# Keeping the row of "same source" flags in bf16 instead of f32: row in memory, preparation tile and scan operand

## The reference, cut to what matters

```
x = ln(x + H W0 + b0)            H = [x, A x, A A x, A A A x]      A z = segment_sum(w * z[dst], src)
x = ln(x + mlp([x, sum, max, mean of the edges' attributes by dst, u]))
x = ln(x + attention over the edges by dst + skip)
x = ln(x + (x + 3 A x) / 4)
```

## The kernel before, in words

| stage | about (us) | what runs in it |
|---|---|---|
| preparation | 0 to 400 | sorting, flags, index tables |
| node rows alone | 400 to 880 | first 48 node groups |
| A | 880 to 1780 | 100 node groups, and the first product (gathers from `in_x_rows`) for 100 edge groups |
| B | 1780 to 2540 | the last 52 node groups, and the second product (gathers from `Z1E`) for 100 edge groups, two for each node group |
| C | 2540 to 3740 | rows of sources: third product (gathers from `Z2E`), layers 1 and 2, attribute scans |
| D | 3740 to 4850 | rows of destinations |
| attention | 4850 to 6050 | third layer |
| last | 6050 to 7560 | fourth layer: gathers, product, scatters |

## Time and profile before

### The profile page before, as it was taken

One profiled execution on the slowest core, in us unless ns is written; L12 is line 12 of the kernel. 1 busy time (PEld: TensorE's weight loads), 2 busy tenths in 40 slices (PEclk: granted clock), 3 DMA queues, 4 the chain that ended last, 5 costly groups with the idle time before them and its releaser, 6 DMA issues.

```text
span 7577.1 us, 104573 instructions
## 1 busy us (share of the span) xinstructions
PE 4996.8 (66%) x26540; PEld 3423.6 (45%) x26540; DVE 4566.0 (60%) x8424; ACT 2745.5 (36%) x5600; POOL 4815.5 (64%) x4823
## 2 busy tenths in 40 slices
PE   0088799997777799999888988777777611111111
PEld 0055566665555677777644444444444311010100
DVE  8855577776666688888533333588888732222222
ACT  0044455554444344444322222377777500000000
POOL 0054566644656576666477777577777677777777
PEclk9999999999999899999899999888888755555555
DMA  0022466666999798888655555433333322222221
GB/s 15 13 82 84 116 196 195 196 197 170 217 224 219 209 257 252 252 250 251 173 155 148 150 154 155 118 108 107 109 109 107 85 65 66 65 66 65 66 65 57
DMA packets 871313, 1058.31 MB, mean 140 GB/s; under 512 B 144418, under 2 KB 505776, under 8 KB 871078
## 3 DMA queue, kind: packets, MB, share of 16 engines
q1 hardware_dynamic: 717578, 805.42, 34.4%
q0 software_dynamic: 153600, 251.49, 16.2%
HBM read 613.72 MB, written 454.66 MB: 141 GB/s over the span
## 4 chain that ended last, share of the span: by engine, by line
DVE 26%; PE 24%; issue 16%; POOL 16%; ACT 7%; DMA 6%; DVEq 5%; SPq 1%; ACTq 0%; POOLq 0%
PE bank L942 10%; POOL gat L645 7%; PE bank L844 5%; POOL xT L645 5%; DVE x L1661 4%; POOL out_rows L658 4%; PE bank L928 3%; DVE ln3vr L1649 2%; DVE t L1722 2%; ACT mbuf L1085 2%; PE bank L931 2%; DMA Z2E<-zE 2%; DMA gat<-X,d_x 2%; PE bank L930 2%; DVEq L1838 2%
## 5 line engine op out<-in xcount | busy, mean ns | idle before, releaser
L844 PE MATMUL bank<-ident,gat 128*128 128x128 f32 x2400 | 452.4, 319 | 1476.1 <-DVE zT L1690 1370.3
L1085 ACT ACTIVATE mbuf<-t 128x512 f32<-128x512 f32 x500 | 315.7, 631 | 2094.3 <-DVE t L1902 1351.9
L844 PEld LDWEIGHTS bank<-ident,gat 128*128 128x128 f32 x2400 | 311.8, 165 | 1633.2 <-issue 1285.3
L942 PE MATMUL bank<-W2s,hT 128*128 128x128 f32 x6400 | 875.7, 293 | 0.0
L1671 DVE TENSOR_TENSOR gat<-gat,pays 128x512 f32<-128x512 f32 x400 | 273.0, 682 | 993.4 <-DMA gat<-X,pays 955.2
L942 PEld LDWEIGHTS bank<-W2s,hT 128*128 128x128 f32 x6400 | 796.6, 203 | 94.5 <-issue 94.5
L928 PE MATMUL bank<-x1T,W1x 128*128 128x512 f32 x1600 | 803.5, 615 | 25.1 <-ACT x1T L1077 16.2
L671 POOL DMA_INDIRECT pays<-PAY,s_q x400 | 379.4, 948 | 626.2 <-DMA PAY<-payl 338.0
L844 PE MATMUL bank<-ident,x 128*128 128x128 f32 x3200 | 512.0, 284 | 236.1 <-DVE x L1661 231.3
L645 POOL DMA_INDIRECT gat<-in_x_rows,pays x400 | 395.0, 987 | 369.7 <-PE bank L844 264.9
L1141 ACT ACTIVATE hT<-bank,b1u 128x512 f32<-128x512 f32 x800 | 506.6, 687 | 256.8 <-PE bank L931 251.8
(11 more groups left out here) (342 smaller groups left out, 11849.2 us busy)
## 6 DMA issues: line engine op xcount, KB each, us to landing
X<-x SPq DMA_DIRECT2D x700, 256.0 KB, 3.9
fB<-row_s_same SPq DMA_DIRECT2D x400, 256.0 KB, 5.3
xT<-in_x_fm SPq DMA_DIRECT2D x200, 256.0 KB
out_rows<-x SPq DMA_DIRECT2D x200, 256.0 KB
ffB<-rows_last_notlast SPq DMA_DIRECT2D x100, 512.0 KB
Z1T<-zT SPq DMA_DIRECT2D x100, 256.0 KB, 2.1
Z1E<-zE SPq DMA_DIRECT2D x100, 256.0 KB
Z2T<-zT SPq DMA_DIRECT2D x100, 256.0 KB, 10.0
```

Source lines behind the costliest of these rows:

```text
L844: mm = pe.transpose(dst[:, t, :], tiles[t], ident[:, :])
L942: mm = pe.matmul(bMLP[:, t, :], hT[h][s][:, t * P:(t + 1) * P], W2s[:, h, :], start=False, stop=h == HC - 1, skip_group_check=True)
L1085: act.activation(sq[k % 3][s % 2], [bT1, t2[s], bSK, t2[s]][k][:, :, :], ACT.Square).then_inc(S(f"squared{k}", s), 1)
```

## The change

The flag row is kept in bf16, two bytes instead of four. 0 and 1 are exact in bf16. Four places change: the row in HBM, the preparation tile `ssame` that the comparison writes and SP stores, the tile that is loaded, and the scan's first operand. The loaded tile is a new one, `sB` (four buffers of 1 KB in each partition), because `fB` keeps its 4-byte use. `fB` stays as it was for the other uses.

```
-        ROWS["s_same"] = dram("row_s_same", [1, E_PAD])
+        ROWS["s_same"] = dram("row_s_same", [1, E_PAD], BF16)
...
-        sold, ssame, sout, sq_f = (early(n, [P, LF]) for n in ("sold", "ssame", "sout", "sq_f"))
+        sold, sout, sq_f = (early(n, [P, LF]) for n in ("sold", "sout", "sq_f"))
+        ssame = early("ssame", [P, LF], BF16)
...
+        sB = slots("sB", [P, G], BF16)
...
-                    row_load(fB[s], ROWS["s_same"], i * SL + s, S("ld_row", s))
+                    row_load(sB[s], ROWS["s_same"], i * SL + s, S("ld_row", s))
...
-                    dve.tensor_tensor_scan(zT[s][:, :], fB[s][:, :], flat(bIN), zT[s - 1][:, G - 1:G],
+                    dve.tensor_tensor_scan(zT[s][:, :], sB[s][:, :], flat(bIN), zT[s - 1][:, G - 1:G],
```

## The result

The changed kernel takes 7551.9 us in the median of 9 runs (7539.04 to 7572.83), against 7573.18 us before (9 runs). The ratio is 0.9972, with a 95% interval of 0.9961 to 0.9984: 21 us or 0.28% faster. In a later comparison it took 7541.1 us against 7573.5, ratio 0.9963 (0.9949 to 0.9977). The forecast was 7550. Two single runs of the later comparisons, of 9712 and 9482 us, were disturbed and are left out of the medians.

What follows compares the result with a forecast made beforehand. Only stage B was taken as bound by transfers, DMA 0.99 full. From 7579.2 us, 24 us of gain leaves 7555; the profiled run lies 5.5 above the median, so 7550 us, own range 7536 to 7560, 8 in 10 within 7512 to 7578.

Steps and rivals of the forecast that it cites:

- What bounds stage B: Stage B alone is held by transfers: DMA busy 0.99 of 640 us, PE 500 us.
- The size of a half load: Each halved flag load in stage B frees 0.25 to 0.39 us of all sixteen engines; 0.32 taken, 31 us for 97.
- A large fixed part: Lower end for stage B's loads: 22 ns fixed per packet, from stages A and C, so 0.25 us saved a load.
- A quarter given back: In stage B the gathers take back a quarter of the 31 us freed by waiting longer, leaving 24 us gained.
- Nothing elsewhere: In stages A, C and last, 300 smaller flag loads cost and gain nil, since DMA is not full there.
- the nine register operations: On SP's queue, 7 us in all and 1.8 us in stage B, on a queue that mostly waits: nil.
- The scan: All 400 scans on VectorE stay at 1271 ns with a bf16 operand, as the product showed no difference by type.
- The third rival: Mixed types slow the scan, so VectorE paces stages A and C: 116 us lost there, 7666 us; chance 0.05.
- The gathers absorb it: Reads of one zero row pace stage B: gain 0 to 12 us, 7568 us; chance 0.24, shared with packets no shorter.
- The gathers shrink too: Stage B's gathers are slowed by q1's traffic and shrink with it: 59 us gained, 7515 us; chance 0.09.
- three times as long: A gather from `Z1E` in stage B keeps an engine so long: 181 us a MB against 69 and 55 in C and last.

Runs made afterwards that it cites:

- many zero rows: Edges with nothing to read spread over 256 zero rows instead of row 0: changed kernel 7475.8 us (0.9870 to before); kernel before, four-byte flags, 7463.2 us (0.9865).
- 16 partitions: Changed kernel with stage B's flags loaded into 16 of 128 partitions only: 7526.6 us, ratio 0.9940 to the kernel before.
- double loads: Kernel before with each four-byte flag load of stage B issued a second time into an unread tile: 7612.3 us, ratio 1.0060 to before.

## Why the prediction was right

**What bounds stage B.** Right. All of the change's effect is there, and it is there only while the DMA engines are full. On the slow chip (shares of 0.72 to 0.85) and with many zero rows (0.79 and 0.87) fewer or more flag bytes moved the stage by 1 to 3 us.

**The size of a half load.** The forecast took 0.32 us, between 0.25 by a fixed part for each packet and 0.39 by bytes, 31 us over 97 loads. The pair of profiles of before and after gave 30.5 us, which looks better than it is, because the kernel before's stretch held less of the other traffic. With equal packets it is 33.3 us, 0.35 us a load. From four bytes to one at equal packets, q1 has 19.36 MB and 860 us less, 44 us for a MB more or less, against 47 to 48.5 for all its bytes together. So there is little room for a fixed part, and the byte end of the range was the nearer one. A large fixed part, as worked out from stages A and C, was wrong: by it a MB more or less would be 30.5 us. Stage C is dearer for another reason, which is open. A share is rounded to 0.1%, 10 us of engine time a step, so this rests on several kernels agreeing, not on one.

The Trainium skill (DMA: Bandwidth & Descriptors, § Anatomy of one DMA) has the moved bytes at 436 GB/s and a constant. It gives both for transfers that GpSimd issues, and the flag loads are SP's. The estimate from it was 29 us. The runs' price of 47.7 us a MB is 21 GB/s for an engine, 335 GB/s for sixteen, lower than the page's figure, and no run here shows the constant.

**A quarter given back.** The size holds on the mean, and the reason isn't shown. Two profiles with four bytes in stage B (633.3 and 625.5 us) and three with two (607.4, 606.6 and 599.3) differ by 25.0 us in the mean, for 32.8 us of engine time: 0.76 is seen. Single pairs give anything from 0.54 (625.5 to 607.4) to 1.10 (633.3 to 599.3). The forecast had the gathers hold the engines longer with more of them in flight. A quarter of 31 us would be 124 us of q0's 4702 us, or 2.6%, and the profiles with whole loads of four or two bytes scatter from 173 to 184 us a MB whichever the flags are, so this can't be seen. The 186 us with 16 partitions is hardly outside that scatter; only the 147 with double loads is. Against the one profile of the kernel before, the share of engine time that the stage shows is 0.85 for the change, 0.81 with 16 partitions, 0.70 with one byte and 0.54 for double loads. With some 8 us between like profiles the first three are not apart. The last, where 8 us are 0.09, is probably lower.

**Nothing elsewhere.** Right: no gain with two bytes in A, C and last, stages C and last within 3 us, the nine register operations not to be seen.

**The scan.** Right: 1271 ns in f32 and bf16, 1270 in uint8. The third rival never came near.

**The rivals.** "The gathers absorb it" is out as a statement on this change, and half right about the stage: the one zero row's reads are what makes it full, and with double loads they gave back nearly half. "The gathers shrink too" would have made stage B 59 us shorter and the kernel 7515 us; neither came. The prices that spoke against it, 69 us a MB in stage C and 55 in the last, are those of queues that carry other transfers beside the gathers, so "three times as long" compared unlike things; the run with 256 rows, 178 to 69, makes the comparison in one stage.

**Chance.** The first comparison's gain of 21 us and the later one's 32 lie on both sides of the forecast's 24. Stage B alone varies by some 8 us between like profiles, and what follows the last gather from `Z2E` took 3915 to 3936 us in the profiles of the faster chips without regard to the flags. That the median came within 2 us of the forecast is luck; a gain of 21 to 32 us is what the runs bear out. The chip is luck too: on the slow one two bytes in stage B gained nothing, and the forecast had no term for that.

## What to carry to other kernels

Work out what a byte costs in DMA engine time (share x 16 x stretch over MB) in the stretch where the engines are full, and count only the loads that run there; elsewhere half the bytes are worth nothing. Then compare that price between queues and stages: the queue that costs three times as much for a MB is the find, and here it was worth three to five times the change. Missing entries that all point at one row of a table can make that row a bottleneck, as in stage B and not in stage C; give them many rows. And a forecast that rests on "the engines are full" holds for the chip on which that was read.

## What the runs showed of the hardware

- Reads of one row. With an estimated 0.61 of the gathers' indices (from the sizes) on one 512-byte row of HBM a MB of gathers took 173 to 186 us of engine time in stage B (147 with double flag loads); with the same indices over 256 rows it took 63 to 69. On the slow chip it was 122 to 137 with one row. In stage C the same step took all of q0 from 67 to 56 us a MB.
- The scan takes the same time with any of three types of its first operand: 1271, 1271, 1270 ns for 4, 2 and 1 bytes, 512 elements.
- The price of a MB in q1 was 47 to 48.5 us with flag packets of 2048, 1024 and 512 bytes and one zero row, and 48.3 and 50.3 us with 256.
- A chip on which the same program takes 15% longer. TensorE there has gaps between matmuls of one group, ahead of which it waits for nothing in the profile. TensorE in order of time in stage C, two bytes in B only, slow chip (start us, us, and in brackets the idle time before):

```profile
3324.44 0.50 PE L896 MATMUL bank<-W0I,zin 128*128 128x128 f32 x3
3325.87 0.36 PE L896 MATMUL bank<-W0I,zin 128*128 128x128 f32 x1 [0.94 <-issue]
3327.28 0.39 PE L896 MATMUL bank<-W0I,zT 128*128 128x128 f32 x2 [1.04 <-issue]
3328.00 0.27 PE L891 MATMUL bank<-W0I,xT 128*128 128x128 f32 x1 [0.33 <-issue]
```

In the brackets stand 0.94, 1.04 and 0.33 us of idle with the releaser "issue". Stage C takes 1437 to 1455 us there and 1127 to 1132 on the others; stage A 1286 to 1306 and 959 to 962. The granted clock in stage B was 0.90 to 0.92 there, and 0.92 for the kernel before on its chip. In stage C it was 0.93 to 0.94 (3100 to 4000 us) against 1.00 (2700 to 3600 us), and 0.80 to 0.81 over the whole span against 0.84 to 0.85. Whether the lower clock comes of the gaps or both of something else is open, and so is what makes the gaps; no run was made on it.
